# Decoder of four layers on one core: projection taken earlier in the all-head attention stages, division ahead in layer 2, scores as pairs of banks

## The reference

```python
x = x + L0_attn(layernorm(x))      # 16 heads of 8, causal, biases, LoRA on the projections
x = x + L0_xattn(layernorm(x), ctx)  # 16 heads of 8, "trinity" mask, biases
x = x + L0_ffn(layernorm(x))
...                                # layer 1: stick-breaking attention, one-head cross attention, experts
x = x + L2_attn(layernorm(x))      # 16 heads of 8, causal, rotary embedding
...                                # layer 2: one-head cross attention, experts; layer 3: dilated one-head attention
x = x + L3_xattn(layernorm(x), ctx, ctx, mask)
...                                # 16 heads of 8, mask from memory; relu(heads @ wo.T + wo_b); then experts

scores = jnp.einsum('bhqd,bhkd->bhqk', qh, kh) + mask
weights = jax.nn.softmax(scores, axis=-1)
ctx = jnp.einsum('bhqk,bhkd->bhqd', weights, vh)
```

## Time and profile before

| | |
|---|---|
| median of 3 runs | 1747.38 us (1746.98 to 1747.76) |
| the profiled execution | 1735.4 us, its span 1733.7 us |
| PE matmul / PE weight load | 1339.4 us (77%) / 827.9 us (48%) |
| DVE / ACT / POOL | 946.9 us (55%) / 918.7 us (53%) / 400.3 us (23%) |
| mean granted TensorE clock | 0.879 of full speed |
| stage L0a | about 56 to 386 us |
| stage L2a | about 946 to 1139 us |
| stage L3x | about 1394 to 1611 us |

### The profile page before, as it was taken

The page is one execution under the profiler, slowest core; times in us unless marked ns, Lnnn a source line. Parts: engine busy times, 40 slices in busy tenths (PEclk is TensorE's granted clock), DMA queues, the critical chain, the costliest instruction groups (busy, mean ns, idle before and its releaser), DMA issues. The chain is left out here.

```text
span 1733.7 us, 27918 instructions
## 1 busy us (share of the span) xinstructions
PE 1339.4 (77%) x9137; PEld 827.9 (48%) x9137; DVE 946.9 (55%) x3708; ACT 918.7 (53%) x2185; POOL 400.3 (23%) x490
## 2 busy tenths in 40 slices
PE   5888888868899999777996888765083577878574
PEld 3455555545444444553564555454062444444464
DVE  4577767754455555444112776647223657666432
ACT  2688877762477766532421666732020467767232
POOL 4433333210311110100004332101544042210134
PEclk9899989999999999877998898886596879989687
DMA  7900000000000000000005000000222000000012
GB/s 207 141 2 2 2 2 1 2 1 1 1 1 1 1 1 1 1 1 1 1 1 179 1 1 2 1 1 12 61 69 79 1 19 13 12 8 1 10 58 78
DMA packets 60263, 42.34 MB, mean 24 GB/s; under 512 B 13188, under 2 KB 54120, under 8 KB 60120
## 3 DMA queue, kind: packets, MB, share of 16 engines
q1 hardware_dynamic: 54752, 32.42, 7.9%
q0 software_dynamic: 3552, 7.33, 1.2%
q10 hardware_dynamic: 1816, 0.81, 0.2%
HBM read 25.88 MB, written 14.66 MB: 23 GB/s over the span
## 5 line engine op out<-in xcount | busy, mean ns | idle before, releaser
L792 ACT ACTIVATE L0a_e<-L0a_e,L0a_neg_max 128x256 f32<-128x256 f32 (+1 forms) x512 | 190.6, 447 | 19.4 <-DVE L0a_neg_max L868 19.4
L679 PE MATMUL L0a_psE<-ident,L0a_e 128*128 128x128 f32 x768 | 121.9, 288 | 16.8 <-DVE L0a_probs L877 8.2
L1216 DVE CUSTOM_DVE_ANT_0 L3x_e<-L3x_psS,L3x_mask_rows 128x256 f32<-128x256 f32 x256 | 92.9, 420 | 64.3 <-PE L3x_psS L1076 64.3
L679 PEld LDWEIGHTS L0a_psE<-ident,L0a_e 128*128 128x128 f32 x768 | 86.9, 145 | 70.5 <-issue 35.9
L1164 ACT ACTIVATE L3x_e<-L3x_e,L3x_neg_max 128x256 f32<-128x256 f32 x256 | 110.7, 503 | 12.7 <-DVE L3x_neg_max L1216 12.7
L792 ACT ACTIVATE L2a_e<-L2a_e,L2a_neg_max 128x128 f32<-128x128 f32 (+1 forms) x256 | 95.2, 445 | 33.6 <-DVE L2a_neg_max L868 33.6
L1084 PE MATMUL L3x_psE<-ident,L3x_e 128*128 128x128 f32 x512 | 81.9, 292 | 28.2 <-DVE scores_L_experts_L L1226 13.8
L868 DVE CUSTOM_DVE_ANT_0 L2a_e<-L2a_psS,causal_rows 128x128 f32<-128x128 f32 (+1 forms) x256 | 76.1, 353 | 36.9 <-PE L2a_psS L669 31.5
L868 DVE CUSTOM_DVE_ANT_0 L0a_e<-L0a_psS,trinity 128x128 f32<-128x128 f32 (+1 forms) x256 | 75.1, 352 | 37.3 <-PE L0a_psS L669 33.3
L868 DVE CUSTOM_DVE_ANT_0 L0a_e<-L0a_psS,causal_rows 128x128 f32<-128x128 f32 (+1 forms) x256 | 75.3, 352 | 35.2 <-PE L0a_psS L669 31.6
L568 POOL TENSOR_SCALAR L0a_km<-L0a_kT,quad_rows 128x256 f32<-128x256 f32 x64 | 57.9, 922 | 155.2 <-ACT L0a_kT L785 155.2
(11 more groups left out here) (652 smaller groups left out, 3231.7 us busy)
## 6 DMA issues: line engine op xcount, KB each, us to landing
L2f_rows<-packed_rows SPq DMA_DIRECT2D x8, 325.0 KB
packed_rows<-zeros SPq DMA_DIRECT2D x1, 2560.0 KB, 30.3
experts_L_L<-in_L_ffn_w_dram SPq DMA_DIRECT2D x1, 2048.0 KB, 8.4
unpacked_rows<-zeros SPq DMA_DIRECT2D x1, 2048.0 KB, 19.9
scores_L_experts_L<-in_L_ffn_w_dram SPq DMA_DIRECT2D x1, 2048.0 KB, 7.8
L2f_back_rows<-unpacked_rows SPq DMA_DIRECT2D x16, 128.0 KB, 2.5
L3x_mask_rows<-in_mask_Bx1xSxS_ff_dram SPq DMA_DIRECT2D x8, 256.0 KB, 2.7
sorted_rows<-zeros SPq DMA_DIRECT2D x1, 1472.0 KB, 19.7
```

The lines of the kernel that those rows point to most:

```text
L679: last = nc.tensor.transpose(psE[i % 2][:, c * P:(c + 1) * P], e[:, i % RING, c * P:(c + 1) * P], mem.ident[:])
L792: last = nc.scalar.activation(at, at, ACT.Exp, bias=neg[:, i % RING, j:j + 1], scale=-1.0)
L1216: last = nc.vector.tensor_tensor_reduce(out=e[:, i % RING, j * S:(j + 1) * S], in0=psS[r][:, j * S:(j + 1) * S], in1=mrow[:, b % 2, t, :], ...
```

## The change

- `settle_x` is split in all three stages. The part that empties psO stays `settle_x`; the statistics become `measure_x`. In `quad_heads` settle_x moves from n = 3 to n = 2, measure_x stays at n = 3. In `masked_heads` settle_x holds only the addition into proj and moves to n = 1; it raises a new semaphore `s_taken`, for which weigh now waits in place of `s_x`; measure_x at n = 3 does relu, the addition to x and the statistics.
- In `quad_heads` three steps move one item ahead: keep_raw to n = 6 (DVE), spread_sums to n = 5 (PE), invert to n = 7 (ACT).
- With rope (layer 2) POOL's divide stands between combine and variants. In layer 0 its place is as it was.
- In `quad_heads` a group's scores are issued as two pairs: strips 0 and 1 at item r = 3, two groups ahead, and strips 2 and 3 at r = 1, one group ahead, as the whole group was. A pair waits for the two reductions that read its two tensors.

```diff
@@ POOL, quad_heads
                 for b in range(NB):
+                    if b + 2 < NB and rope:
+                        combine(b + 2)
+                    if b > 0 and rope:
+                        divide(b - 1)
                     if b + 2 < NB:
-                        if rope:
-                            combine(b + 2)
                         variants(b + 2)
                     if biased:
                         add_bias(b)
-                    if b > 0:
+                    if b > 0 and not rope:
                         divide(b - 1)
@@ PE, quad_heads
-                def score(group):
+                def score(group, half):
                     b, g = divmod(group, GROUPS)
                     if group >= 1:
-                        pe.wait_ge(s_red, 4 * group)
-                    if g == 0:
+                        pe.wait_ge(s_red, 4 * group - 2 + 2 * half)
+                    if g == 0 and half == 0:
                         pe.wait_ge(s_km, b + 1)
-                    for r in range(4):
+                    for r in (2 * half, 2 * half + 1):
...
-                        score(0)
+                        score(0, 0)
+                        score(0, 1)
                     values(b)
                 turn(2)
+                score(1, 0)
...
+                        if r == 3 and i + 5 < LAST:
+                            score(i // 4 + 2, 0)
                         if r == 1 and i + 3 < LAST:
-                            score(i // 4 + 1)
+                            score(i // 4 + 1, 1)
...
-                        if n == 6 and b > 0:
+                        if n == 5 and b > 0:
                             spread_sums(b - 1)
@@ ACT, quad_heads
-                    if n == 8 and b > 0:
+                    if n == 7 and b > 0:
                         invert(b - 1)
@@ DVE, quad_heads
                     nc.vector.tensor_tensor(xb, xb, psO[:, 0:S].rearrange("p (t d) -> p t d", t=TPB), ALU.add).then_inc(s_x, 1)
+
+                def measure_x(b):
                     dve.wait_ge(s_x, b + 1)
...
+                    if n == 2 and b >= 2:
+                        settle_x(b - 2)
                     if n == 3 and b >= 2:
-                        settle_x(b - 2)
+                        measure_x(b - 2)
                     if n == 4 and b + 2 < NB:
                         keep_h(b + 2)
-                    if n == 7 and b > 0:
+                    if n == 6 and b > 0:
                         keep_raw(b - 1)
@@ PE, masked_heads, weigh
                         if b >= 1:
-                            pe.wait_ge(s_x, b)
+                            pe.wait_ge(s_taken, b)
@@ DVE, masked_heads
                 def settle_x(b):
                     dve.wait_ge(s_out, b + 1)
                     dve.wait_ge(s_rows_kept, 1)
+                    if b >= 1:
+                        dve.wait_ge(s_x, b)
+                    nc.vector.tensor_tensor(proj[:], psO[:, 0:S].rearrange("p (t d) -> p t d", t=TPB),
+                                            out_bias[:].unsqueeze(1).to_broadcast([P, TPB, D]), ALU.add).then_inc(s_taken, 1)
+
+                def measure_x(b):
                     xb = mem.x[:, b * TPB:(b + 1) * TPB, :]
-                    steps.step(nc.vector.tensor_tensor(proj[:], psO[:, 0:S].rearrange("p (t d) -> p t d", t=TPB),
-                                                       out_bias[:].unsqueeze(1).to_broadcast([P, TPB, D]), ALU.add))
+                    dve.wait_ge(s_taken, b + 1)
                     nc.vector.scalar_tensor_tensor(xb, proj[:], 0.0, xb, ALU.max, ALU.add).then_inc(s_x, 1)
...
+                    if n == 1 and b >= 2:
+                        settle_x(b - 2)
                     if n == 3 and b >= 2:
-                        settle_x(b - 2)
+                        measure_x(b - 2)
```

## The result

The changed kernel takes 1685.2 us against 1747.5 us (medians of 4 runs each, 1684.1 to 1687.2 and 1747.0 to 1747.8), a ratio of 0.9645 with a 95% interval of 0.9628 to 0.9662: 62 us faster. The forecast was 32 us faster, 1715 in a range of 1690 to 1741. The sign was right, the size half of what came, and the time lies 5 us under the range.

The account below looks back on a forecast made before the run. No engine was full in the three stages; PE stood waiting, with low clock behind its holes, and would be fullest after. Layer 0 0, layer 2 -14, masked heads -18: -32 us, 1747.4 to 1715, range 1690 to 1741.

Parts of the forecast that it names:

- a bank of layer 0: Quad heads of layer 0: 16.45 + 3.55 for pairs + 0.15 of waits, 20.15 us; stage sum 0, between -5 and +14.
- a bank of layer 2: Quad heads of layer 2: 17.5 of PE plus 3.55 and 0.15, 21.2 us; stage sum -14, between -8 and -17.
- the low clock that was left in the masked heads: Masked heads, layer 3: of 8.4 us of low clock over six periods, two thirds taken as gone, 5.6 us.
- the 12 us between the profiled execution and the median: Whole kernel: the median lies 12 us above the profiled 1735.4; the same difference was taken off 1747.4, giving 1715.
- the 5 us of loss that it put into two ramps: Layers 0 and 2: ramp and last bank of each were taken to lose 2.5 us.
- The holes: PE waits of 1.99 us ahead of weigh (layer 0), 2.95 ahead of project (layer 2), 2.14 in masked heads would go.
- The echo: Layer 0: right after the hole the granted clock falls to 0.50, costing a bank 1.59 us.
- A pair costs what a group costs: Scores, layers 0 and 2: each pair 1.06 us; with form changes 3.55 us of PE a bank, 85 us in all.
- Rival 1: Scores: a pair takes 0.86 us, not 1.06; 29 us come on top, 1686. Chance 0.08.
- Masked heads: Layer 3: period falls by 2.14 us, 24.57 to 22.4; with 5.6 of low clock 18 us gained, between 11 and 21.
- Rival 2: Layers 0, 2, 3: clock stays low once a bank, 6 us slower, 1753, chance 0.09; in half of them 1735 to 1745, 0.08.
- Rival 3: DVE, waiting in its queue for project and weigh, holds back reductions; each 0.5 us past 1.8 slack costs 16, 1731. Chance 0.10.

Follow-up runs that it names:

- a_settle3: Changed kernel with settle_x of quad_heads back at n = 3; 1679.4 us, ratio 0.9812 to the kernel before on the same chip.
- a_divide_late: Changed kernel with POOL's division behind km again in layer 2; 1681.2 us, ratio 0.9828 to the kernel before on the same chip.
- b_masked: Kernel before with the change of masked_heads alone; 1683.8 us, ratio 0.985 to the kernel before on the same chip.
- b_split: Kernel before with the split of the scores into pairs alone; 1712.9 us, ratio 1.0025 to the kernel before on the same chip.
- a_whole: Changed kernel with whole score groups at r = 1 again; 1631.6 us, ratio 0.9546 to the kernel before on the same chip.
- a_ring_late: Changed kernel with keep_raw, spread_sums and invert back at n = 7, 6, 8; 1650.4 us, ratio 0.9645 to the kernel before.
- w_ring_late: Changed kernel with whole score groups at r = 1 and keep_raw, spread_sums, invert at n = 7, 6, 8; 1651.4 us, ratio 0.9455 to the kernel before.
- b_again: Kernel before, unedited, run and traced again with the experiments; 1708.8 us, ratio 0.9996 to the kernel before on the same chip.
- a_again: Changed kernel, unedited, run again on another chip; 1649.5 us, ratio 0.9642 to the kernel before on that chip.
- w_r0_settle1: Changed kernel with whole groups at r = 0, keep_raw, spread_sums, invert at n = 7, 6, 8, quad_heads' settle_x at n = 1; 1672.3 us, ratio 0.9575.
- w_settle1: Changed kernel with whole groups at r = 1, keep_raw, spread_sums, invert at n = 7, 6, 8, quad_heads' settle_x at n = 1; 1605.0 us, ratio 0.9388.

## Why the prediction was right or wrong

**The step that failed is the sizing of the sum, not its mechanism.** The forecast was 32 us, 62 came, and the time lies under the range. The terms that were mis-sized: a bank of layer 0 (20.15 us, 19.31 measured), a bank of layer 2 (21.2, 19.99 measured), the low clock that was left in the masked heads (2.8 us, none measured, and 2.7 us of gain in a period that wasn't counted), and the 12 us between the profiled execution and the median, which were carried over as a constant. The account of the 30 us that were missing, by the first pair of traces: without the 5 us of loss that it put into two ramps, the forecast for the three stretches is 37 us, and they gave 60.3 (some 11 more than forecast in layer 0, 6 in layer 2, 6 in the masked heads). The rest of the span got 12.0 us longer where those 5 were allowed, 7 the other way. And the offset made 14.

**The holes: right in kind.** The waits ahead of weigh and of project are gone, the clock is 1.00, and a bank of layers 0 and 2 is PE's own length. a_settle3 and a_divide_late bring each wait back by itself and are 30 and 32 us slower; b_masked alone gives 27.

**The echo: right that it goes, but the hole alone doesn't decide it.** In layer 0 of b_split a hole of 1.20 us is left in every bank and the clock is 1.00; in a_settle3 the same hole brings the low clock in 2 of 14 banks. And without pairs, with a hole of 0.54 us, a_whole has 1.00 too. So in layer 0 either part is enough for the clock: the split alone, or the earlier steps alone.

**A pair costs what a group costs: right.** 1.06 us in the rows above, as the pair of layer 1 in the earlier trace rows. Rival 1, 0.86 a pair by a full matmul's time, fell. The Trainium skill's span model (TensorE: Matmul & The Clock Gate, Part 3) gives one matmul's time and a few ns for each more. The few ns agree (1.06 us for two, 1.07 for four); that the one matmul takes what a matmul of 128 rows takes doesn't, for that is 0.86 here. Its rule that only matmuls beside each other gain holds, and this trace agrees: by a_ring_late and w_ring_late the split is a loss of 22.9 and 6.1 us in the two stages.

**The bank of layer 0: 20.15 expected, 19.31 measured.** The base of 16.45 was meant as PE's busy time in the earlier trace rows, which is 16.37 (0.08 too much). The six pairs of the measured bank take 6.35 us, so all its other steps take 12.96. The busy 16.37 less three groups of 1.07 leaves 13.16 for them, 0.20 more. Most of that is waits that no idle time shows, since a matmul's modelled end covers part of them; this is read from a comparison of the two timelines and has no run of its own. In the bank of the earlier trace rows that has clock 1.00, turn of h lasts 0.51 us until the next start, and values 0.63:

```profile
104.87 0.61 PE L655 MATMUL L0a_psM<-wT_L_attn,L0a_hT 128*128 128x128 f32 x4
105.50 0.63 PE L679 MATMUL L0a_psE<-ident,L0a_e 128*128 128x128 f32 x4
...
110.24 0.38 PE L628 MATMUL L0a_psM<-ident,L0a_h 128*128 128x128 f32 x2
110.75 0.63 PE L679 MATMUL L0a_psE<-ident,L0a_e 128*128 128x128 f32 x4
```

In the timeline of after they last 0.27 and 0.54. (Of the 0.24 that turn of h lasts longer, 0.13 stand as idle time after it; the rest is hidden.) The other terms that were too large are the 3.55 for pairs and their change of form (3 x 1.06 and no more fits, some 0.4) and 0.15 for waits of which there are none. Together 0.84, over 12 to 14 banks some 11 us. The forecast for the stage with its ramp was 0. By the first traces 10.9 came (13.3 less 2.4 of a later first weigh), by b_again and a_again 13.6. How much of the later start is the change's doing is open: in three traces with the same code of layer 0 (before, b_again, b_masked) the first weigh stands at 75.7, 73.1 and 77.3.

**Layer 2: 21.2 expected, 19.99 measured.** The same three terms, and the 17.5 from a bank at clock 0.93, of which 16.81 were left. With the ramp 14 us were expected, without it 16.5; the stretch gave 22.7.

**Masked heads: 18 expected, 24.3 came** (26.6 against the second trace of before, which has 2.3 us more of low clock). The period of 22.4 was right to 0.04. I had left a third of the low clock in, and nothing for the seventh period, which has no wait for the addition but had low clock (23.95, now 21.25).

**The base of the whole sum.** 1747 less 1735 was carried over as a constant. It wasn't one: the changed kernel's profiled execution lies 2 us above its median, hence the 14 us. The other 16 are the difference between the profiled executions, 48.3 where 32 were forecast. By b_again and its runs the kernel before is longer when its clock falls more often, and the change takes the low clock away in these three stages. Which banks made up the 12 us on the first chip no trace shows; between its trace and b_again's 5.4 us lie in the stretches (3.1 in L0a, 2.3 in L3x).

**The rivals.** Rival 2 (the clock stays low once a bank) was the opposite of what happened; it had 0.09, and 0.08 for its half. The only rival that would have made the kernel faster than the forecast was the cheap pair, and it set the range's lower end. That the bases of the banks could be too large, or the 12 us of offset go, was among no rivals. Rival 3 (DVE's new waits in its queue) did not come true at n = 2: the slack was 0.8 us by the trace (193.13 to 193.94) and not 1.8, still enough. In w_r0_settle1, one item sooner with the scores sooner as well, it did, at 0.53 us a bank.

**"What the split buys I cost at nothing": too little.** By a_ring_late and w_ring_late a bank costs 1.62 us more with the pairs (19.13 against 17.51), while their PE time is 3.18; the other 1.56 are waits that the pairs take away. With invert at its new place they take away more still: a_whole's bank is only 0.66 us shorter than the changed kernel's. None of this touches the forecast of 20.15, in which PE was full anyway, but it is why the kernel without the split doesn't reach 16.4 by itself. w_settle1, with settle_x one item sooner still, comes nearest at 16.88.

## What to carry to other kernels

A wait on the fullest engine can be worth more than its length when the clock falls behind it: look whether it does (holes of 2.4 us brought it down each time in a_divide_late, holes of 1.2 us seldom in a_settle3), and where it does, price the wait plus the low stretch, and allow in the range for the low clock of the whole stage to go. Read how much an engine needs from the start-to-start times of instructions that follow one another without a wait, not from its busy time. And check the parts of a change one by one in the kernel that results: two of this change's parts (the pairs, and the earlier invert) cost time that the others had earned, and the second could be seen only with the first taken back.

## What the runs showed of the hardware

Two matmuls of 32 rows on two strips of the array take 1.06 us for 512 float32 columns, and four on four strips 1.07; one of 128 rows takes 0.86 (206.12 to 206.98 in the earlier trace rows). In these traces the strips are slower than the full array by a quarter, whether two or four are used.

The granted clock fell at or right behind some holes of PE and not at others. Holes of 2.37 us ahead of project in layer 2 of a_divide_late: in all 5 banks. Holes of 1.99 us ahead of weigh in layer 0 of the kernel before: in 12 of 14. Of 1.94 us ahead of project in layer 2 of b_split: in 2 of 5. Of 1.20 us ahead of weigh in layer 0 of a_settle3: in 2 of 14. Each time it went to 0.50 of full speed.

The time of the kernel before varies over 12 us in 29 runs on one chip, along with the granted clock (0.884 to 0.877). The changed kernel may be steadier, its four runs span 3.0 and 3.4 us on two chips; but four runs of the kernel before on the first chip span 0.8, and with so few runs it isn't shown. And the same kernel differs by 36 us from chip to chip, in the parts of the span behind layer 2's and behind layer 3's stage (16 us each, at a DMA share of 0.12 to 0.17 and a clock of 0.73 to 0.81), outside the three stages studied here; its cause wasn't looked into.
